# Another set of written orders for the five engines of a two-layer attention and experts kernel

## What is computed

```python
def _L0_attn_ref(x, ...):        # linear attention, 16 heads of 8
    q = elu(q) + 1; k = elu(k) + 1
    out = (q @ (k.T @ v)) / (q @ k.sum() + 1e-6)
    return out @ w_proj.T + b_proj
def _L0_ffn_ref(x, ...):         # 8 experts, top 2 per row, F = 512
    combine, idx = _top2_gate(xn, Wg)
    h = gelu(xn @ w1 + b1e); y = h @ w2 + b2e
    return x + sum(g * y)
def _L1_attn_ref(x, ...):        # softmax attention, 8 heads, dk = 16, S = 512
def _L1_ffn_ref(x, ...):         # 8 experts, top 1, one 128 x 128 matrix each
    return x + expert_out[chosen]
h = layernorm(x) * (1 + ca) + sa
x = x + ga * _L0_attn_ref(h)
h = layernorm(x) * (1 + cb) + sb
x = x + gb * _L0_ffn_ref(h)
...
```

## Time and profile before

| | |
|---|---|
| device time, 3 runs | 694.29, 697.45, 696.57 us; median 696.57 |
| span of the profiled execution | 694.9 us (its own device time isn't listed apart) |
| PE busy | 602.8 us, 87% (its fillers, 47.9, included) |
| DVE busy | 484.6 us, 70% |
| ACT busy | 390.7 us, 56% |
| POOL busy | 334.6 us, 48% |

### The profile page before, as it was taken

How to read it: one execution, slowest core, us unless ns; L and a number is a source line. 1 busy time by engine, 2 the same in 40 slices (tenths; PEclk the granted TensorE clock), 3 DMA queues, 4 the chain that set the end, 5 groups by cost and what they waited for, 6 DMA issues and landing times. The chain is left out here.

```text
span 694.9 us, 11955 instructions
## 1 busy us (share of the span) xinstructions
PE 602.8 (87%) x3825; PEld 385.3 (55%) x3825; DVE 484.6 (70%) x1275; ACT 390.7 (56%) x866; POOL 334.6 (48%) x363
## 2 busy tenths in 40 slices
...
GB/s 338 100 1 0 62 107 152 179 241 258 190 292 322 175 312 262 138 323 199 214 132 193 208 282 245 76 39 188 56 53 1 166 62 190 130 80 34 31 61 30
DMA packets 47037, 106.40 MB, mean 153 GB/s; under 512 B 7056, under 2 KB 22224, under 8 KB 45440
## 3 DMA queue, kind: packets, MB, share of 16 engines
...
q10 hardware_dynamic: 432, 0.34, 0.2%
...
## 5 line engine op out<-in xcount | busy, mean ns | idle before, releaser
L889 ACT ACTIVATE bufa<-PS 128x512 f32<-128x512 f32 x256 | 139.5, 599 | 78.5 <-PE PS L1556 72.0
L1200 DVE TENSOR_REDUCE mxs<-PS 128x2 f32<-128x1024 f32 x128 | 151.2, 1218 | 28.9 <-PE PS L1540 28.1
L848 ACT ACTIVATE bufb<-PS,bufb 128x128 f32<-128x128 f32 x368 | 103.5, 380 | 43.2 <-PE PS L1505 42.9
L1505 PE MATMUL PS<-bufb 128*128 128x128 f32 x736 | 97.2, 281 | 14.0 <-DMA bufb<-in_experts_dram 7.0
L1505 PEld LDWEIGHTS PS<-bufb 128*128 128x128 f32 x736 | 90.5, 195 | 20.9 <-issue 9.0
L1513 PE MATMUL PS<-bufb 128*128 128x128 f32 x736 | 97.3, 281 | 0.4 <-ACT bufb L848 0.3
L701 POOL DMA_INDIRECT bufb<-slots_out,bufb x64 | 62.2, 971 | 68.9 <-DMA bufb<-slots_out,bufb 36.0
L688 POOL DMA_INDIRECT slots_in<-bufb x64 | 67.2, 1049 | 56.9 <-DVE bufb L1146 38.7
L1513 PEld LDWEIGHTS PS<-bufb 128*128 128x128 f32 x736 | 91.3, 197 | 3.8 <-issue 1.4
L1540 PE MATMUL PS<-stk 96*128 96x512 bf16 x256 | 75.2, 386 | 16.1 <-DVE mxs L1200 5.6
L1556 PE MATMUL PS<-stk 108*128 108x512 bf16 x256 | 81.4, 389 | 7.8 <-ACT bufa L889 6.8
...
## 6 DMA issues: line engine op xcount, KB each, us to landing
bufb<-in_experts_dram SPq DMA_DIRECT2D x92, 514.0 KB, 5.1
...
```

What stands on the lines that cost most here:

```text
L848: last = nc.scalar.activation(hs[:, n % HR, fc, :], ps[:, P * fc:P * fc + P], ACT.Gelu_apprx_tanh, bias=ws[:, n % WR, F + fc:F + fc + 1])
L889: nc.scalar.activation(probs[:, i % PR, j, :], psum("s2", i, j), ACT.Exp, scale=DH1 ** -0.5)\
L1200: nc.vector.tensor_reduce(mxs[:, gr % 2, 2 * j:2 * j + 2, h], psum("s1", i, j).rearrange("p (c n) -> p c n", c=2), axis=AX.X, op=ALU.max)\
L1505: last = nc.tensor.matmul(ps[:, P * fc:P * fc + P], ws[:, n % WR, P * fc:P * fc + P], xq[:, q % 2, P * x:P * x + P], start=True, stop=True)
```

## The change

Only the text of `ORDERS` changes. All five lists are written in another order and PE's items get other banks; each list has the same items as before (a word of SP's list, `ldv.0.0`, that no branch handles, is gone). The filler stays 41.7 us in sum by the list and at the same items. Two lines of the diff, POOL's:

```diff
-        an1.0.0 an1.1.0 anx.0.0 bn1.0.0 anx.1.0 bn3.0.0 an1.2.0 bsc.0.0 bn1.1.0 bsc.0.1 bsc.0.2 bsc.0.3 an1.3.0 bn3.1.0 anx.2.0
...
+        an1.0.0 anx.0.0 an1.1.0 bn1.0.0 bn3.0.0 an1.2.0 anx.1.0 bsc.0.0 bsc.0.1 bsc.0.2 bsc.0.3 bn1.1.0 an1.3.0 anx.2.0 bn3.1.0
```

273 lines of the change are left out of this document (136 added, 137 removed).

## The result

Measured: 676.22 us, median of 5 (675.24 to 680.74), against 696.42 (693.7 to 697.45) of the kernel before in the same job: ratio 0.9728, interval 0.9695 to 0.9762. In a later job the changed kernel ran once more: 675.38 against 694.94, ratio 0.9669, interval 0.9621 to 0.9717. That ratio leaves out the two longest of the six executions (spans 677.5 and 681.7), which count as slow because they lie over 1.5% above the shortest; over all six it is 0.972. So it is 19 to 23 us faster; the forecast was 686 with a range of 672 to 699.

A forecast was written before the change was run, and what follows sets the result against it. PE, losing time to waits, was taken to bound the first 440 us, DVE the rest. Terms -6.9 - 3.5 - 4 + 4 + 0 = -10.4 took the 694.9 us span to 684.5; plus 1.7 gives 686, range 672 to 699.

The forecast's parts named there:

- Term 1: Up to the first experts (gate, scatter, load, first expert): three parts on one chain, -6.9 us, bounds 0 to -9.1.
- (a): DVE's normalise of `bn2.0` no longer clashes with POOL's X += on the shared ports: -2.4 us, or 0.
- (b): A POOL norm moves behind pair 0's 16 scatters; only pair 1's gate waits for it: -2.0 us, or 0.
- (c): First `bh` items: with `apr.2` ahead, the 2.96 us wait for ACT mostly goes: -2.5 us, ends 0 and -4.7.
- Term 2: 181 to 318 us: 14.2 us of PE waits, most of them exchanged for later ones: -3.5 us, ends 0 and -14.2.
- exchange at `btr.3`: Most of the 6.13 us wait at 244 us comes back at `btr.3`, about 5 us; 1 us is won.
- Term 3: At 380 us: `s1.16`'s 3.14 us wait for SP's `cst.2.0` goes, with lost clock: -4 us, ends 0 and -4.8.
- Term 4: Expert weights: less PE work between `by` and a later `bh` makes short waits: +4 us, ends +1.5 and +14.
- Term 5: 440 us to the end: DVE sets the pace with the same work: 0 us, ends -5 and +5.
- The moved waits (1): Rival: waits at ends of POOL chains only move; 698 us, or 693 with the front's gain kept; chance 0.21.
- The slow weights (2): Rival: weights become the bound at `bh` in pairs 1 to 3, +22 us, giving 704 us; chance 0.14.
- Both long waits (3): Rival: both long waits between 181 and 318 us really go, -14.2 there, giving 673.5 us; chance 0.14.

The follow-up runs named there:

- hybrids: Four kernels mixing the lists of the kernel before and the changed kernel, cut at a moment; ratios to before 0.9874, 0.9829, 0.9785 and, late part new only, 0.9985.
- first_experts_new: New order up to the end of pair 0's experts, old order from there on; 683.17 us, ratio to the kernel before 0.9829 (0.9761 to 0.9898).
- scatter_alone: Kernel before, with only POOL's norm `bn1.1` moved behind all 16 scatters of pair 0; 711.49 us against 698.18, ratio 1.0177.
- apr2_behind: Changed kernel, with `apr.2` back behind the second `bh` on PE; 678.17 us, ratio to the kernel before 0.9757.
- cpt0_back: Changed kernel, with `cpt.0` back behind the gathers of pair 1 on POOL; 677.4 us, ratio to the kernel before 0.972.
- cpt0_middle_alone: Kernel before, with only `cpt.0` moved into the middle of pair 1's gathers on POOL; 705.77 us, ratio 1.0117.

## Why the prediction came out as it did

The direction and the range held; the gain was about twice the forecast. By its own terms (the hybrids' ratios times 696):

- **Term 1, -6.9; measured about -12** (7 to 17 by the interval of first_experts_new). This is the step that failed in size. In the two profiles the first slot transposition comes 6.7 us earlier (112.02 and 105.28), where (a) and (b) had 4.4, and from there to `anm.3` 7.5 more are won, where (c) had 2.5.

  (a) The clash is gone from `bn2.0` (2.14 for 4.53), but that won only 0.6 us: `an2.1`, which had covered POOL's square root, now stands ahead, and DVE waits 1.75 us for it. The positions are 4.1 us earlier all the same. 2.3 of these I hadn't seen: `pm.0.0` goes ahead of `atr.0.0`, and its 3.8 us of filler with it, into a time in which PE had to wait for x anyway. PE's `aq.0` comes at 20.18 for 22.52; in the other profiles it comes at 17.62 to 20.44 with the new front and at 21.14 to 22.07 with the old, so in most executions the launch wins more than the pair shows. I counted fillers as unmoved because their sum was; no run moves this one alone, and the last 1.2 of the 4.1 aren't traced.

  (b) 3.4 us for 2.0 in the scatter. scatter_alone shows that the norm's move alone shortens it by 4, but also that the sentence on what waits for that norm was wrong: behind DVE's `bn2.1` stood not only the gate of pair 1 but the attention of pair 2, so the time is won only with DVE's move, which I had set down as a side effect.

  (c) The wait of 2.96 is gone, by the lists because the second `bh` no longer needs the bank of `bxt.0.1` (apr2_behind). The rest of the 7.5 is what the term left out: from the first `bh` to `anm.3` PE's idle time fell from 5.8 to 1.8 us in all, and the grant rose from 0.97 to 1.00, worth about 2 us (an estimate: 66.9 us x 0.03):

```profile
113.79:180.67 66.88, 61.05 (x483) 56.83 (x482) 35.67 (x118) 52.42 (x131) 33.57 (x27) 0.97 0.64 209
107.50:166.46 58.96, 57.12 (x471) 53.74 (x470) 39.63 (x133) 47.86 (x127) 31.94 (x25) 1.00 0.71 228
```

- **Terms 2 to 4, -3.5 -4 +4; measured together about -3.** Term 2 (from the start of `anm.3` to that of `ctr.1`): 137.73 us before, 133.55 after, -4.2. The size is right in part by luck, for the way was another. The exchange at `btr.3` didn't come: POOL's chain there was as I summed it (`btr.3` 70.1 us behind `anm.3`, 68.7 before), but PE had been given more work ahead of it. The wait for weights went, and waits came ahead of `ctr.1`, though at the banks of the scores and not at `ctr.1`; that `cpt.0`'s place exchanged the one for the others is not shown (cpt0_back), and the move works only with DVE's `cpq.0` (cpt0_middle_alone), which the term left out. Term 3: the wait at `s1.16` is gone, but the term had its cause wrong. The earlier trace rows put it down to DVE's L1194, here `cpv.3`:

```profile
379.60 0.68 DVE L1194 TENSOR_TENSOR vv<-PS,bv 128x512 f32<-128x512 f32 x1
```

That item empties the pair of banks which `s1.16` fills, and it had stood behind a combine that waited 3.32 us for a gather; SP had begun `cst.2.0` at 366.21, 14 us ahead, and such a reload lands after 5.1 us in the median. In the new order `cpv.3` stands ahead of that combine. Of the -4 nothing is seen: the lead is 18.4 us at `ctr.1`, 18.2 at `by.3.0` (371.41 and 353.23), and 21.4 at the last expert tile, some 3 of them attention not yet done (an estimate from the rows of these items). Term 4: seven short waits of 4.1 us in sum where two of 7.0 stood, 6.6 of them the one of term 2: +3.7 for the +4 taken (eight waits of 6.1 us in the changed kernel's later profile, so +5.7 there). The Trainium skill ("DMA: Bandwidth & Descriptors", section "Issuing engines are not separate DMA queues") says that transfers share 16 engines and interleave. That this stretches the loads where gathers run, no run here shows: the longest new waits, in cpt0_back, came from a late issue, and the sum is far from the +14 of the upper end.
- **Term 5, 0; measured -1 alone, about -4 behind the new order.** The intervals leave it open which.
- **The clock.** I counted 1.7 us for it, in term 3, and gave term 1 nothing. By the mean grants up to 6.5 us of the gain are the clock's: fewer waits, fewer stretches at the lower level. It is not a term of its own but lies in those above, in term 1 above all (the launch, and the stretch behind the first `bh`), and the profiled pair hides part of it. No run here changes the clock alone, so how large its part is stays open.
- **Rivals.** The moved waits (1): new ones of 7.8 us stand at the scores, but the time up to there shrank all the same. The slow weights (2) exist at a sixth to a quarter of the price (3.7 to 5.7 of 22 us). Both long waits (3) are gone, but of its -14.2 for term 2 only 4.2 came; that its 673.5 was nearer than 686 is luck, since term 1 brought what term 2 lacked. A slip in rival 1: with term 1 kept it sums to 693.7, so 694, not 693.
